# A fused attention and feed-forward block on one core: the transposes of the probabilities and of the next batch's x move from TensorE to the DMA queue, and the scores stay in PSUM

## The chip, the cores and the metric

One core of a Trainium2 chip runs the whole program in one launch. The metric is device time in microseconds (us). The kernel before takes 2261.73 us (median of 3 runs, 2261.62 to 2261.98).

## The reference

Input `x` is 8 x 512 x 1024 in f32. Attention has 16 heads of 64 with rotary position, a causal mask and a softmax; the feed-forward part is one 1024 x 1024 product with bias and a LoRA term (rank 16, one of 3 adapters by batch).

```
x = x + layernorm(attention(layernorm(x), Wq, Wk, Wv) @ Wo)
x = x + layernorm(layernorm(x) @ W.T + bias + lora(layernorm(x)))
attention: q, k rotated; softmax(where(causal, q k^T, -1e9) / 8) v
```

## The kernel before, in words

Every f32 operand of a product is split into a high and a low fp16 part, and each product is three fp16 matmul passes (high high, high low, low high) that add up in PSUM. Constants of the program are powers of two that keep the parts in range.

**Two phases.** Phase 1 does attention for 8 batches; for each batch there are 8 slots, one for each pair of heads, so 64 slots `g = 8 b + p`. Phase 2 goes over 32 tiles of 128 tokens: `Wo`, layer norm, feed-forward, layer norm. Batch 0 and batch 7 are written out; batches 1 to 6 are a loop of two bodies. The slot is a function of each engine's program (`slot(b, kind, p)`), so the order on each engine is the order in which it is written there, and semaphores tie the engines.

**One slot before, by engine (lines of the kernel before):**

- TensorE: the scores of pair p (L460, 24 matmuls of 128 to 512 columns, two heads at a time), the q product of the next pair (L435 to L437, 24 matmuls), in slots 1 to 4 of batches 0 to 6 eight f32 transposes of the next batch's normalised x (L425), the k product of the next pair (24 matmuls), the product of the probabilities with v for the previous pair (L480, 24 matmuls), 20 f32 transposes of this pair's probabilities (L469), and a quarter of the v product (L446 to L448, 24 matmuls). The v product is not there in slots 0 to 3 of batch 0 and in slots 4 to 7 of batch 7.
- VectorE (DVE): for eight score blocks ("units": 4 query blocks of 128 times 2 heads, widths 512, 384, 128, 256) the mask, the scale and the row's extreme in one pass from PSUM to SBUF (L807); the low part of v (L692); the reciprocal of the row sums (L722); the drain of q (L698, L699: a product with the cosines and a shuffle of partitions); layer-norm statistics of the next x tile (L669 to L674) and the low parts of its transposes (L686); the drain of k; `qk_low` of q (L705), the low part of the output (L716), five low parts of the transposed probabilities (L711), `qk_low` of k (L705), and the normalised x (L679).
- ScalarE (ACT): the high part of v (L989), eight exponentials with their row sums in SBUF (L1050), and the high parts: x (L984), q and k (L996), output (L1005), probabilities (L1000).
- GpSimd (POOL): eight multiplications of the exponentials by the reciprocals (L1131), the rotation of q and of k (two f32 passes each, L1122 and L1124), and one power for the layer norm (L1118).
- SP: issues all DMAs: the next x tile and the store of a pair's output (L335). In batch 7 it loads `Wo` at slot 0 and the feed-forward weight at slot 6, and at slot 7 what phase 2 needs (`phase2_loads`, with the first attention output at L331).

The scores of slot g + 1 wait for `qk_low` of k, the last link of the chain: k product, DVE drain, POOL rotation, ACT high part, DVE low part. In batch 7 the maxima of the two late weights are taken (L620, two passes of 2048 columns in each of two slots), GpSimd reduces them over the partitions (L1114), and the weights are split (ACT L978, DVE L663).

Of the kernel before, what the change touches and what calls it, by code (L numbers as in the profile page):

```python
# [52 lines left out]
Q_ORDER = (3, 2, 0, 1)  # L53
S_OFF = {3: 0, 2: 512, 0: 896, 1: 1024}
S_LEN = 1280
UNITS = [(j, a) for j in Q_ORDER for a in range(2)]
# [6 lines left out]
PT_GROUPS = (  # L63
# [5 lines left out]
)  # L69
PT_ROW = {0: ((0, 0), (2, 0)), 1: ((1, 0), (3, 0)), 2: ((4, 0), (4, 256)), 3: ((1, 384), (3, 384))}  # L70
NG = len(PT_GROUPS)

BANK_O = 7
BANK_XT = (5, 6)
# [15 lines left out]
W_V, W_Q, W_K, W_O, W_F = range(5)  # L90


def sandwich_kernel(nc, x, wq, wk, wv, wo, wf, bias, lora_a, lora_b, starts, consts, out):
# [7 lines left out]
    with ExitStack() as ctx:  # L101
# [12 lines left out]
        raw2 = arena2[:, :].rearrange("p (k n) -> p k n", k=KT)  # L114
        raw_r1 = region[1][:, :, :, :].rearrange("p k h n -> p (k h n)").bitcast(F32).rearrange(
            "p (k n) -> p k n", k=KT)
        w_raw = {W_V: raw1, W_Q: raw_r1, W_K: raw1, W_O: raw2, W_F: raw2}

        x_ring = arena2[:, 0:4096].rearrange("p (t d) -> p t d", t=ST)

# [5 lines left out]
        scores = arena1[:, 4096:4096 + 2 * S_LEN].rearrange("p (a n) -> p a n", a=2)  # L126
        pt = half(arena1[:, 6656:6656 + 2 * S_LEN], ("p (h g q) -> p h g q", dict(h=2, g=NG)))
# [15 lines left out]
        row_sum = sb("row_sum", [PART, 8], F32)  # L143
        row_inv = sb("row_inv", [PART, 8], F32)
# [72 lines left out]
        exp_done = sem("exp_done")  # L217
        inv_done = sem("inv_done")
        norm_done = sem("norm_done")
        pt_done = sem("pt_done")  # L220
        pt_high = sem("pt_high")
        pt_low = sem("pt_low")
# [83 lines left out]
        def unit_sb(j, a):  # L306
            return scores[:, a, S_OFF[j]:S_OFF[j] + 128 * (j + 1)]

# [4 lines left out]
        def _(sp):  # L313
            def load_raw(w, c):
                sp.dma_start(w_raw[w][:, KC * c:KC * (c + 1), :],
                             raw_dram[w][:, KC * c:KC * (c + 1), :]).then_inc(raw_in[w][c], 16)
# [33 lines left out]
            def slot(b, kind, p):  # L350
                first, last_b = kind == 0, kind == B - 1
                g = 8 * b + p
                if not last_b and p < ST:

                    sp.wait_ge(xt_done, 8 * b + 2 * p + 2)
                    sp.dma_start(x_ring[:, p, :], x_v[b + 1, p]).then_inc(x_in[p], 16)
                if last_b and p == 0:

                    sp.wait_ge(xt_done, 8 * B)
                    sp.wait_ge(qk_done[1], PAIRS * (B - 1))  # L360
                    sp.wait_ge(v_done, 8 * (B - 1))
                    for c in range(CHUNKS):
                        load_raw(W_O, c)
                if last_b and p == 6:
                    for c in range(CHUNKS):

                        sp.wait_ge(w_low_done, CHUNKS * W_O + c + 1)
                        load_raw(W_F, c)
                if last_b and p == PAIRS - 1:
                    phase2_loads()  # L370
                if not (first and p == 0):

                    sp.wait_ge(o_low, g)
                    if p == 0:
                        store_o(b - 1, PAIRS - 1, 1)
                    else:
                        store_o(b, p - 1, (p - 1) % 2)

# [5 lines left out]

            sp.wait_ge(o_low, PAIRS * B)
# [34 lines left out]
        def _(pe):  # L420
# [44 lines left out]
            def p_transposes():  # L465
                for bank, blocks in PT_GROUPS:
                    for n, (a, kt, j) in enumerate(blocks):
                        at = S_OFF[j] + 128 * kt
                        last = nc.tensor.transpose(ps[:, bank, 128 * n:128 * n + 128], scores[:, a, at:at + 128],  # L469
                                                   ident)  # L470
                    last.then_inc(pt_done, 1)

            def pv_products(pair):

                for kt in range(ST):
                    n = S - 128 * kt
                    for hl, vl in ((0, 0), (0, 1), (1, 0)):
                        for a in range(2):
                            grp, c = PT_ROW[kt][a]
                            last = mm(ps[64 * a:64 * a + 64, BANK_O, 128 * kt:S],  # L480
                                      v_split[:, kt, 2 * pair + a, HD * vl:HD * vl + HD], pt[:, hl, grp, c:c + n],
                                      start=(kt == 0 and hl == 0 and vl == 0), stop=(kt == ST - 1 and hl == 1))
# [27 lines left out]
            def slot(b, kind, p):  # L510
# [10 lines left out]
                need(pe, pt_low, NG * g)  # L521
# [4 lines left out]
                if has_qk:  # L526
                    if p == PAIRS - 1:
                        need(pe, xt_low, 8 * b + 16)
# [698 lines left out]
```

## Time and profile before

| | us |
|---|---|
| median of 3 runs | 2261.73 |
| the profiled execution, its own time | 2262.72 |
| its span in the trace | 2260.9 |
| TensorE busy, share of the span | 2151.5, 95% |
| VectorE busy | 1386.0, 61% |
| ScalarE busy | 791.6, 35% |
| GpSimd busy | 773.7, 34% |
| granted TensorE clock, mean | 0.978 |

The page of the profile has busy times, then the span in slices, then the chain of work that ended last, then the costliest groups. Busy time says which engine is nearly full, the slices say where, and a timeline of one slot says which wait ends last there.

### The profile page before, as it was taken

What the parts mean: (1) busy time and instruction counts of PE and PEld (TensorE: products, weight loads), DVE (VectorE), ACT (ScalarE), POOL (GpSimd) and SP (SyncE); (2) the same over time, 40 slices, a digit from 0 to 9 for tenths busy, and PEclk for the clock granted to TensorE, in tenths of its full rate; (3) what the DMA queues carried; (4) which work ended last, traced back from release to release, by engine and by line L of the source; (5) the groups of instructions that cost most, each with busy time, mean ns of one, the idle gap of its engine ahead of it and who ended that gap; (6) DMA issues with size and microseconds to landing.
All of it is one profiled execution on the core that took longest, in us unless ns stands there. A gap on an engine that the chain in (4) does not pass through costs nothing.

```text
span 2260.9 us, 35372 instructions
## 1 busy us (share of the span) xinstructions
PE 2151.5 (95%) x12928; PEld 1104.9 (49%) x12928; DVE 1386.0 (61%) x3295; ACT 791.6 (35%) x1797; POOL 773.7 (34%) x905
## 2 busy tenths in 40 slices
PE   3979999999999999999999998779999999999997
PEld 1445555555555555555555554444444444444443
DVE  6776566676576576566567565675555555555554
ACT  4544444444344444444444443532111111111111
POOL 0245455464554545455454544520000000000000
PEclk8999999999999999999999999979999999999999
DMA  7000010010010010010001020041433333423232
GB/s 294 1 29 15 20 43 11 24 34 19 24 31 24 10 43 24 10 44 20 15 29 33 15 85 10 20 177 47 121 94 84 97 82 97 117 64 114 62 79 56
DMA packets 98772, 125.47 MB, mean 55 GB/s; under 512 B 71745, under 2 KB 71745, under 8 KB 97570
## 3 DMA queue, kind: packets, MB, share of 16 engines
q1 hardware_dynamic: 98594, 123.12, 18.0%
q8 instruction: 109, 1.79, 0.3%
q14 instruction: 69, 0.57, 0.1%
HBM read 72.77 MB, written 33.55 MB: 47 GB/s over the span
## 4 chain that ended last, share of the span: by engine, by line
PE 90%; DVE 5%; issue 2%; POOL 1%; DMA 1%; ACT 1%; SPq 0%; POOLq 0%; DVEq 0%; ACTq 0%
PE ps L568 29%; PE ps L435 10%; PE ps L436 9%; PE ps L437 9%; PE ps L469 6%; PE ps L460 5%; PE ps L446 5%; PE ps L448 5%; PE ps L447 5%; PE ps L480 5%; PE ps L590 1%; PE ps L425 1%; POOL arena L1131 1%; DVE arena L711 1%; DVE w_part L620 1%
## 5 line engine op out<-in xcount | busy, mean ns | idle before, releaser
L1131 POOL TENSOR_TENSOR arena<-arena,row_inv 128x512 f32<-128x512 f32 (+3 forms) x512 | 357.9, 735 | 651.2 <-DVE row_inv L722 651.2
L435 PE MATMUL ps<-arena,region 128*128 128x512 f16 x1024 | 389.5, 380 | 0.0
L436 PE MATMUL ps<-arena,region 128*128 128x512 f16 x1024 | 388.9, 380 | 0.0
L437 PE MATMUL ps<-arena,region 128*128 128x512 f16 x1024 | 388.5, 379 | 0.0
L568 PE MATMUL ps<-region 128*128 128x512 f16 x1536 | 341.2, 383 | 8.5 <-ACT arena L1083 4.6
L807 DVE CUSTOM_DVE_ANT_0 arena<-ps,con,pow 128x512 f32<-128x512 f32 (+3 forms) x512 | 246.5, 547 | 162.1 <-PE ps L460 161.9
L568 PE MATMUL ps<-region,arena 128*128 128x512 f16 x1536 | 337.3, 379 | 0.0
L1050 ACT ACTIVATE arena<-arena,neg_max 128x512 f32<-128x512 f32 (+3 forms) x512 | 280.0, 548 | 99.3 <-DVE neg_max L807 99.3
L698 DVE TENSOR_TENSOR rotated<-ps,con 128x512 f32<-128x512 f32 x128 | 88.5, 691 | 266.7 <-PE ps L437 266.7
L568 PEld LDWEIGHTS ps<-region 128*128 128x128 f16 x1536 | 151.2, 99 | 193.5 <-issue 10.3
L1083 ACT ACTIVATE arena<-ps,sm 128x1024 f32<-128x1024 f32 x64 | 77.0, 1204 | 477.2 <-DVE sm L883 477.2
L568 PEld LDWEIGHTS ps<-region,arena 128*128 128x128 f16 x1536 | 149.2, 98 | 174.1 <-issue 0.8
L996 ACT ACTIVATE qk_high<-rotated 128x512 f16<-128x512 f32 x128 | 82.6, 645 | 422.8 <-POOL rotated L1124 422.8
L1167 POOL TENSOR_TENSOR sm<-sm,con 128x1 f32<-128x1 f32 x64 | 35.1, 548 | 508.1 <-DVE sm L876 508.1
L446 PE MATMUL ps<-region,arena 128*128 128x512 f16 x512 | 195.0, 381 | 11.8 <-DVE region L663 11.8
L711 DVE SCALAR_TENSOR_TENSOR arena<-ps,arena 128x512 f16<-128x512 f32 x320 | 196.5, 678 | 0.0
L447 PE MATMUL ps<-region,arena 128*128 128x512 f16 x512 | 195.1, 381 | 0.0
L448 PE MATMUL ps<-region,arena 128*128 128x512 f16 x512 | 194.9, 381 | 0.0
L1122 POOL TENSOR_TENSOR swapped<-swapped,con 128x512 f32<-128x512 f32 x128 | 173.3, 1354 | 43.5 <-DVE swapped L699 35.9
L1124 POOL TENSOR_TENSOR rotated<-rotated,swapped 128x512 f32<-128x512 f32 x128 | 173.4, 1355 | 10.0
L866 DVE BATCH_NORM_STATS2 st<-ps 128x6 f32<-128x512 f32 x128 | 82.8, 689 | 151.9 <-PE ps L568 140.6
L1000 ACT ACTIVATE arena<-ps 128x512 f16<-128x512 f32 x320 | 163.4, 609 | 4.5 <-PE ps L469 4.5
(121 smaller groups left out, 2668.2 us busy)
## 6 DMA issues: line engine op xcount, KB each, us to landing
arena<-x SPq DMA_DIRECT2D x32, 512.0 KB, 3.8
attn_scratch<-o_st SPq DMA_DIRECT2D x64, 256.0 KB, 2.2
region<-attn_scratch SPq DMA_DIRECT2D x8, 2048.0 KB, 8.8
v_split<-x SPq DMA_DIRECT2D x32, 512.0 KB, 4.2
out<-v_split SPq DMA_DIRECT2D x32, 512.0 KB, 5.1
arena<-wv SPq DMA_DIRECT2D x4, 1024.0 KB, 13.6
region<-wq SPq DMA_DIRECT2D x4, 1024.0 KB, 18.6
arena<-wk SPq DMA_DIRECT2D x4, 1024.0 KB, 5.5
```

Source lines behind the costliest of these rows:

```text
L435: mm(o, w[:, k, 0, cols], xnt[par][:, k, 0, :], start=(k == 0), stop=False)
L436: mm(o, w[:, k, 0, cols], xnt[par][:, k, 1, :], start=False, stop=False)
L437: last = mm(o, w[:, k, 1, cols], xnt[par][:, k, 0, :], start=False, stop=(k == KT - 1))
L446: mm(o, xnt[par][:, k, 0, tok], region[2][:, k, 0, cols], start=(k == 0), stop=False)
L447: mm(o, xnt[par][:, k, 0, tok], region[2][:, k, 1, cols], start=False, stop=False)
L448: last = mm(o, xnt[par][:, k, 1, tok], region[2][:, k, 0, cols], start=False, stop=(k == KT - 1))
L568: last = mm(ps[:, bank + c, :], stationary(k, hl), w[:, k, wl, 512 * c:512 * c + 512], start=(k == 0 and hl == 0 and wl == 0), stop=final)
L711: v.scalar_tensor_tensor(pt[:, 1, grp, :], ps[:, PT_GROUPS[grp][0], :], P_UP, pt[:, 0, grp, :], ALU.mult, ALU.subtract).then_inc(pt_low, 1)
L807: v.tensor_tensor_reduce(out=unit_sb(j, a), in0=unit_ps(j, a), in1=causal[:, 512 - width:512], scale=pow2[:, S_NEG:S_NEG + 1], scalar=HIGH ...
L1050: s.activation(unit_sb(j, a), unit_sb(j, a), ACT.Exp, bias=neg_max[:, n:n + 1], scale=-1.0, accum_out=row_sum[:, n:n + 1]).then_inc(exp_do ...
L1124: gp.tensor_tensor(rotated[which][:, :], rotated[which][:, :], swapped[which][:, :], ALU.add).then_inc(rot_done[which], 1)
L1131: gp.tensor_tensor(unit_sb(j, a), unit_sb(j, a), row_inv[:, n:n + 1].broadcast_to([PART, 128 * (j + 1)]), ALU.mult).then_inc(norm_done, 1)
```

## The change

- The 20 transposes of a slot's probabilities leave TensorE. The high and low parts are now formed before the transposition: ScalarE and VectorE read the exponentials in PSUM, multiply by the reciprocal of the row sum (times 2^14) and write fp16 blocks `p_split`; SP then issues two DMA transposes of 128 x 2560 fp16 (20 blocks of 128 x 128 each) into `pt`, after the previous pair's product with v has ended.
- Scores, mask and exponentials stay in PSUM: L842 of the kernel after (L807 before) writes its result where it read it, and the exponential does so too.
- GpSimd's eight multiplications a slot are gone.
- The eight x transposes of slots 1 to 4 leave TensorE: ScalarE makes the high part of the normalised x (1024 columns), VectorE the low part in the next slot, and SP issues two DMA transposes of 128 x 1024 fp16.
- The ring of four x tiles becomes one tile, so that the next x tile is loaded once the low part of the last is made.
- The product with v is cut at block borders: 36 matmuls of 128 or 256 columns for 24 of 128 to 512; the sum of columns is the same.
- The order of the units is (2, 0, 3, 1) by query block; the output bank is 6, which two units of scores also use.
- On VectorE the k drain comes before the statistics of x, and both `qk_low` come after the low part of the output.
- The space for the late weights is halved: two chunks of four at a time. `Wo` chunks 0, 1 load at slot 0 and 2, 3 at slot 1 of batch 7, and 0, 1 again at slot 4; the feed-forward weight's at slots 5 and 6, and 0, 1 again after the last transposes. Their maxima are taken after the low parts of the probabilities, for `Wo` in slots 1 and 2 in place of 0 and 1.

```diff
-Q_ORDER = (3, 2, 0, 1)
+Q_ORDER = (2, 0, 3, 1)
...
+READY = (2, 2, 4, 4, 5, 6, 7, 8)
+PV_PIECES = {0: ((0, 2), (2, 2)), 1: ((1, 1), (2, 2)), 2: ((2, 2),), 3: ((3, 1),)}
...
 SP, slot:
+                    for hl, src in enumerate((xn_high_t, xn_low_t[:, :])):
+                        sp.wait_ge(xn_split[hl], n)
...
+                        sp.dma_start_transpose(xnt[1 - bp][:, :, hl, tok], src).then_inc(xnt_in[hl], 16)
...
+                    sp.dma_start(x_tile, x_v[b + 1, p]).then_inc(x_next_in, 16)
+                if not (first and p == 0):
+                    sp.wait_ge(pv_done, g)
+                for hl in range(2):
+                    sp.wait_ge(p_done[hl], 8 * g + 8)
+                    sp.nop(nofuse=True)
+                    sp.dma_start_transpose(pt[:, hl], p_split[:, hl].rearrange("p a n -> p (a n)")).then_inc(
+                        pt_in[hl], 16)
...
 PE, slot:
-                need(pe, masked, 8 * g + 8)
-                if not last_b and 1 <= p <= ST:
-                    need(pe, xn_done, 4 * b + 4 + p)
-                    for hh in range(2):
-                        x_transposes(p - 1, hh, BANK_XT[hh])
...
                 if not (first and p == 0):
+                    need(pe, p_done[1], 8 * g + 4)
                     need(pe, v_low, v_before(kind, p, b))
+                    for hl in range(2):
+                        need(pe, pt_in[hl], 16 * g)
                     pv_products((p - 1) % PAIRS)
-                need(pe, norm_done, 8 * g + 8)
...
-                p_transposes()
...
 DVE:
+            def p_low_part(g, n):
+
+                j, a = UNITS[n]
+                need(dve, p_done[0], 8 * g + READY[n])
+                v.scalar_tensor_tensor(unit_p(j, a, 1), unit_ps(j, a), row_inv[:, n:n + 1], unit_p(j, a, 0),
+                                       ALU.mult, ALU.subtract).then_inc(p_done[1], 1)
...
-                    v.tensor_tensor_reduce(out=unit_sb(j, a), in0=unit_ps(j, a), in1=causal[:, 512 - width:512],
+                    v.tensor_tensor_reduce(out=unit_ps(j, a), in0=unit_ps(j, a), in1=causal[:, 512 - width:512],
...
+                if not last_b and 1 <= p <= ST:
+                    xn_low_part(4 * b + p - 1)
+                inverse(g)
                 if has_qk:
                     qk_drain(0, g + 1, bank)
...
+                need(dve, pt_in[1], 16 * g)
+                for n in range(len(UNITS)):
+                    p_low_part(g, n)
+                if last_b and p in (1, 2):
+                    part_max(W_O, 2 * (p - 1))
+                    part_max(W_O, 2 * (p - 1) + 1)
...
 ACT, slot:
+                need(act, pt_in[0], 16 * g)
+                for n in range(len(UNITS)):
+                    p_high_part(g, n)
...
+                if not last_b and p < ST:
+                    xn_high_part(4 * b + p)
...
 POOL, slot:
-                for n in range(len(UNITS)):
-                    normalise(g, n)
```

On VectorE, slot 2 of an odd batch (first body of the loop), between the masks and the drain of k, before:

```order
L722 RECIPROCAL row_inv<-row_sum 128x4 [waits exp_done]
L698 TENSOR_TENSOR rotated<-ps,con 128x512 [waits q_done]
L699 STREAM_SHUFFLE swapped<-ps 128x512
...
L669 BN_STATS bn<-arena 128x6 [waits x_in3]
L669 BN_STATS bn<-arena 128x6
...
L686 TENSOR_TENSOR arena<-ps,arena 128x4x128 [waits xt_high]
...
L698 TENSOR_TENSOR rotated<-ps,con 128x512 [waits k_done]
```

and after:

```order
L714 TENSOR_TENSOR xn_low_t<-arena 128x1024 [waits xnt_low_in,xn_high_done]
...
L757 RECIPROCAL row_rec<-row_sum 128x8 [waits exp_done]
L759 TENSOR_SCALAR row_inv<-row_rec 128x8 [waits recip_done]
L732 TENSOR_TENSOR rotated<-ps,con 128x512 [waits q_done]
L733 STREAM_SHUFFLE swapped<-ps 128x512
...
L746 SCALAR_TENSOR_TENSOR arena<-ps,row_inv,arena 128x384 [waits p_high_done]
L746 SCALAR_TENSOR_TENSOR arena<-ps,row_inv,arena 128x128 [waits p_high_done]
...
L746 SCALAR_TENSOR_TENSOR arena<-ps,row_inv,arena 128x256 [waits p_high_done] x2
L732 TENSOR_TENSOR rotated<-ps,con 128x512 [waits k_done]
L733 STREAM_SHUFFLE swapped<-ps 128x512
```

The low part of x and the eight low parts of the probabilities now stand ahead of the drain of k (`rotated` and `swapped`); the statistics (BN_STATS) have gone behind it.

On the SP queue, one slot of the same loop body before (it loads the next x tile and stores the output of the last pair):

```order
L356 ISA [waits xt_done]
L356 DMA arena<-x 128x1024
L335 ISA [waits o_low]
L335 DMA attn_scratch<-o_st 128x1024
```

and after:

```order
L368 DMA_TRANSPOSE arena<-arena 128x8x128 [waits xn_high_done]
L368 DMA_TRANSPOSE arena<-xn_low_t 128x8x128 [waits xn_low_done]
L374 ISA [waits xn_low_done]
L374 DMA arena<-x 128x1024
L376 REGISTER_ALU
L378 ISA [waits pv_done]
L380 DMA_TRANSPOSE arena<-arena 128x20x128 [waits p_high_done]
L380 DMA_TRANSPOSE arena<-arena 128x20x128 [waits p_low_done]
L341 ISA [waits o_low]
L341 DMA attn_scratch<-o_st 128x1024
```

SP now waits for four more events in each such slot and issues four transposes between the load and the store.

## Rows read from the trace of the kernel before

**Rows 1.** Stretches: length, busy PE, PEld, DVE, ACT, POOL; PEclk, DMA share, GB/s.

```profile
98.40:271.60 173.20, 158.78 (x1034) 86.12 (x1035) 112.27 (x298) 74.87 (x202) 88.89 (x100) 0.96 0.06 21
271.60:1323.80 1052.20, 1051.43 (x6913) 562.48 (x6912) 681.16 (x1752) 468.36 (x1248) 532.42 (x600) 1.00 0.08 25
1323.80:1490.70 166.90, 140.20 (x909) 74.23 (x909) 111.24 (x250) 71.01 (x177) 84.19 (x85) 0.93 0.15 58
1490.70:1516.20 25.50, 13.88 (x93) 9.52 (x94) 19.32 (x53) 9.18 (x24) 5.86 (x9) 0.57 0.40 139
```

**Rows 2.** The chain that ended last, in order of time, from one slot's scores on.

```profile
841.64 1.74 PE ps L460 x24
...
848.66 0.87 PE ps L425 x8
...
854.71 1.75 PE ps L480 x24
856.46 2.33 PE ps L469 x20
...
863.98 1.74 PE ps L460 x24
```

**Rows 3.** Timeline of DVE in that slot (start us, us, what, idle before).

```profile
842.64 0.75 DVE L807 CUSTOM_DVE_ANT_0 arena<-ps,con,pow 128x512 f32<-128x512 f32 x1 [2.75 <-PE ps L460]
...
846.41 0.69 DVE L692 SCALAR_TENSOR_TENSOR v_split<-ps,v_split 128x512 f16<-128x512 f32 x1
...
848.70 0.69 DVE L698 TENSOR_TENSOR rotated<-ps,con 128x512 f32<-128x512 f32 x1 [1.51 <-PE ps L437]
...
850.02 1.25 DVE L669 BATCH_NORM_STATS2 bn<-arena 128x6 f32<-128x512 f32 x2
...
854.75 0.69 DVE L698 TENSOR_TENSOR rotated<-ps,con 128x512 f32<-128x512 f32 x1 [1.74 <-PE ps L437]
...
860.73 0.68 DVE L705 TENSOR_TENSOR qk_low<-rotated,qk_high 128x512 f16<-128x512 f32 x1
```

**Rows 4.** Timeline of ACT in that slot.

```profile
843.43 0.72 ACT L1050 ACTIVATE arena<-arena,neg_max 128x512 f32<-128x512 f32 x1 [1.16 <-DVE neg_max L807]
...
847.31 0.49 ACT L1050 ACTIVATE arena<-arena,neg_max 128x256 f32<-128x256 f32 x1
...
857.09 2.56 ACT L1000 ACTIVATE arena<-ps 128x512 f16<-128x512 f32 x5
```

**Rows 5.** Timeline of POOL in that slot.

```profile
857.89 1.27 POOL L1124 TENSOR_TENSOR rotated<-rotated,swapped 128x512 f32<-128x512 f32 x1
```

**Rows 6.** Phase 2's low part of x, whole span (busy us, mean ns).

```profile
L925 DVE TENSOR_TENSOR arena<-arena 128x1024 f16<-128x1024 f32 x32 | 39.2, 1225 | 37.6 <-ACT arena L1093 37.6
```

**Rows 7.** Phase 2: the SP queue's two transposes of 128 x 1024 fp16.

```profile
1604.51 2.60 SPq L396 DMA_TRANSPOSE arena<-arena  x2
```

**Rows 8.** The stretch of a microsecond in which their DMA work ended.

```profile
1608.00:1609.00 1.00, 1.00 (x6) 0.49 (x5) 0.00 (x0) 0.91 (x1) 0.00 (x0) 1.00 0.38 70
```

**Rows 9.** DVE in batch 0, slot 1: masks and q's drain after an idle TensorE.

```profile
120.99 0.75 DVE L807 CUSTOM_DVE_ANT_0 arena<-ps,con,pow 128x512 f32<-128x512 f32 x1 [1.02 <-PE ps L460]
...
129.14 0.69 DVE L698 TENSOR_TENSOR rotated<-ps,con 128x512 f32<-128x512 f32 x1 [4.20 <-PE ps L437]
```

**Rows 10.** DVE in batch 7: maxima of two weight chunks, and the split of two.

```profile
1353.76 4.45 DVE L620 TENSOR_REDUCE w_part<-arena 128x1 f32<-128x2048 f32 x2
...
1455.48 4.73 DVE L663 SCALAR_TENSOR_TENSOR region<-arena,pow,region 128x2048 f16<-128x2048 f32 x2
```

**Rows 11.** POOL in batch 7, slot 2: q's rotation, the reduction, k's rotation.

```profile
1379.18 1.27 POOL L1124 TENSOR_TENSOR rotated<-rotated,swapped 128x512 f32<-128x512 f32 x1
1386.48 0.41 POOL L1114 PARTITION_ALL_REDUCE w_max<-w_pmax  x1 [6.03 <-issue]
1394.06 1.25 POOL L1122 TENSOR_TENSOR swapped<-swapped,con 128x512 f32<-128x512 f32 x1 [7.17 <-issue]
```

**Rows 12.** The chain that ended last, at the end of slot 63.

```profile
1507.17 8.87 DMA region<-attn_scratch
```

More of the change, by code:

```diff
@@ L304, in unit_ps, with unit_p, raw_of @@
             return ps[:, S_BANK[j][a], c:c + 128 * (j + 1)]
-        def unit_sb(j, a):
-            return scores[:, a, S_OFF[j]:S_OFF[j] + 128 * (j + 1)]
+        def unit_p(j, a, hl):
+            return p_split[:, hl, a, S_OFF[j]:S_OFF[j] + 128 * (j + 1)]
+        def raw_of(w, c, again):
+            if w in w_raw:
+                return w_raw[w][:, KC * c:KC * (c + 1), :]
+            return raw_late[c + 2 if w == W_F and again else c % 2]
         block = ctx.enter_context(nc.Block())
@@ L383, in _ @@
             over_batches(sp, batch)
+            for hl in range(2):
+                sp.wait_ge(pt_in[hl], 16 * PAIRS * B)
+            for c in (0, 1):
+                load_raw(W_F, c, again=True)
             sp.wait_ge(o_low, PAIRS * B)
@@ L463, in score_products @@
                         last.then_inc(s_done, 1)
[L465 to L471, printed above, removed]
             def pv_products(pair):
                 for kt in range(ST):
-                    n = S - 128 * kt
                     for hl, vl in ((0, 0), (0, 1), (1, 0)):
[L478 to L482, printed above, removed]
+                        for j, nq in PV_PIECES[kt]:
+                            at = S_OFF[j] // 128 + kt
+                            step = (S_OFF[j + 1] - S_OFF[j]) // 128 if nq == 2 else 1
+                            for a in range(2):
+                                blocks = pt[:, hl, NB * a + at:NB * a + at + (nq - 1) * step + 1:step, :]
+                                last = mm(ps[64 * a:64 * a + 64, BANK_O, 128 * j:128 * (j + nq)],
+                                          v_split[:, kt, 2 * pair + a, HD * vl:HD * vl + HD], blocks,
+                                          start=(kt == 0 and hl == 0 and vl == 0 and j == 0), stop=(kt == ST - 1 and hl == 1))
                 last.then_inc(pv_done, 1)
@@ L538, in slot @@
                 if not (first and p == 0):
+                    need(pe, p_done[1], 8 * g + 4)
                     need(pe, v_low, v_before(kind, p, b))
+                    for hl in range(2):
+                        need(pe, pt_in[hl], 16 * g)
                     pv_products((p - 1) % PAIRS)
-                need(pe, norm_done, 8 * g + 8)
-                if not last_b and 1 <= p <= ST:
-                    need(pe, xt_low, 8 * b + 8 + 2 * p)
-                p_transposes()
                 if v_slot(kind, p):
@@ L556, in _ @@
             over_batches(pe, batch)
-            pe.wait_ge(pt_low, NG * PAIRS * B)
+            for hl in range(2):
+                pe.wait_ge(pt_in[hl], 16 * PAIRS * B)
             pe.wait_ge(o_low, PAIRS * B - 1)
@@ L964, in step @@
                 if kind == 0:
[L965 to L966 removed]
+                    split_low(W_F, 2, LATE_ORDER[2])
+                    split_low(W_F, 3, LATE_ORDER[3])
             over_tiles(dve, step)
@@ L1066, in slot @@
                     o_evac(g - 1, (p - 1) % 2, stored)
-                for grp in range(NG):
-                    pt_evac(grp, g)
                 if has_qk:
                     qk_high_part(1, g + 1)
+                if not last_b and p < ST:
+                    xn_high_part(4 * b + p)
             def batch(b, kind):
@@ L1156, in slot @@
                     rotate(1, g + 1)
+                if not last_b and p < ST:
+                    ln_rstd(p, 4 * b + 4 + p)
             def batch(b, kind):
```

208 lines of the change are left out of this document (104 added, 104 removed), and 5 rows, old and new, of the table PT_GROUPS.

## The prediction

> **What bounds the kernel now.** I read the busy times by stretch first, because the program has parts with different limits. In batches 1 to 6 TensorE is busy 1051.43 of 1052.20 us at full clock, while DVE has 681, POOL 532, ACT 468 [rows 1]: there the kernel is worth exactly the TensorE work in it. Batch 0 (158.78 of 173.20) and batch 7 (140.20 of 166.90) have gaps, and slot 63 with the hand-over to phase 2 is 25.5 us for 13.9 of TensorE work at clock 0.57 [rows 1]. Second, the chain in order of time for one slot: 22.34 us from scores to scores (863.98 - 841.64), of which 0.87 are x transposes, 2.33 the transposes of the probabilities, 1.75 the product with v, 1.74 the scores [rows 2]; the rest is the three projections. Third, timelines of DVE, ACT and POOL in the same slot, to see what the other engines can be asked for when TensorE's share shrinks [rows 3 to 5].
>
> Phase 2 (744.7 us from 1516.2) and the first 98.4 us are touched by nothing that I can price; I leave them.
>
> **The sum against TensorE, batches 1 to 6.** Removed: 48 x 2.33 = 111.8 and 24 x 0.87 = 20.9, together 132.7 us. The product with v gets 36 matmuls for 24 but the same 3840 pairs of columns; the 24 take 1.75 us, 0.46 ns a column, which is 2.4 GHz with nothing to spare for a fixed cost [rows 2]. I take 0 for the cut; at worst 12 more instructions at 0.02 us add 0.24 us a slot (11 us), and that goes into the range. A slot becomes 22.34 - 3.20 = 19.14 us, and one without x transposes the same. So 1052.2 becomes 919.5.
>
> **Does the rest fit into 19.14 us?** Times from the start of a slot (T). Masks start at 1.0 and v's low part follows at 4.77 [rows 3]; nothing says that writing to PSUM costs more, so I keep that. The low part of x, 1024 columns, is priced by phase 2's same pass, 1.23 [rows 6]: about 6.6 with v's part (0.6). Exponentials: the first needs two masks now, so starts near 2.0, and the eight took 843.43 to 847.8, 4.4 us [rows 4]: 6.4. The two small operations of the inverse end near 6.9. DVE would wait for q's product until 7.1 anyway (848.70 - 841.64) [rows 3], so up to here the added work is hidden in an old wait. The drain of q takes 1.32 (848.70 to 850.02) [rows 3]: 8.4. Eight high parts on ACT: 512 columns cost 0.51 [rows 4], and I take 0.85 ns a column and 0.08 to 0.15 each, 3.0 us: 7.0 to 10.0. Eight low parts on DVE at 0.6 us for 512 columns (the v part, 846.41 on, [rows 3]) are 3.2 us: 11.7. The k product ends so that its drain can start at 13.11 - 0.87 = 12.24 [rows 3]. DVE is ready 0.5 us early.
>
> From k's drain to the next scores the old links are: drain start to end of rotation 859.16 - 854.75 = 4.41 [rows 3, 5], a high part (0.6), a low part (0.68 [rows 3]), hand-offs 0.5: 6.2 us. The statistics and both other low parts lie under POOL's rotation. That gives 12.24 + 6.2 = 18.4 for the earliest next scores against TensorE's 19.14: slack **0.7 us**. TensorE stays the bound, but the chain of the k half has come from 3 us behind to 0.7 us behind it.
>
> **The queue.** SP must wait for the end of the previous product with v (T + 14.0) and then issues both big transposes. Sixteen blocks of 128 x 128 were issued in 2.60 us and their DMA work ended about 4.0 us after the first issue (1604.51 to 1608.4) [rows 7, 8]. Forty blocks: by the rate of issue 2.5 x 2.60 + 1.4 = 7.9 us, by plain scaling 10.0 us; I take 9, so landing at T + 23. The first who needs them is ACT's high part of the next slot (the source buffer is free only then) at 26.1, for the high half alone, then DVE's low part at 27.5, then TensorE at 31.3. Spare: 4 us. The x transposes (2.60 us of issue) and the x load sit at T + 1 to 8 of a slot, when the queue is idle; the x tile must land before the statistics at 13.6. The output store waits until about 20.5, and its buffer is needed two slots later. I cost all of it at nothing; if this cover is gone, the rival on transposes says what it costs.
>
> The Trainium skill (DMA: Bandwidth & Descriptors, the table of quirks) gives 261 GB/s for DMA transposes with a non-contiguous middle dimension: an estimate by it is 5.0 us for the 1.31 MB of a slot. It would only widen the spare time; no run here shows that rate, the trace stands at 16 blocks in 4.0 us.
>
> **Batch 0.** Slots 0 to 3 have no v product, so TensorE's work (14.0 us) ends before the chain (18.4), and idle time lowers the clock. In slot 1 before, q's drain came 8.15 us after the masks instead of 6.06 [rows 9, 3]: 2.1 us for a clock at the lower level after an idle gap. I take 18.7 for slot 0, 18.4 + 2.1 for slots 1 to 3, 19.14 + 2.1 for slot 4, and 3 x 19.14: 158.9, which is 14.3 less than 173.2. Bounds: no clock cost, 150; twice the cost, 167.
>
> **Batch 7.** Here the change adds work ahead of k's drain. Slot 0: 19.1. Slot 1: two maxima of 4.45 us [rows 10] come after the low parts, 11.7 + 4.4 = 16.1 for the drain, + 6.2 = 22.3 (21.5 before, when they filled an old wait). Slot 2: maxima again until 16.3; POOL's gap of 6.03 us before the reduction starts when q's rotation ends, now T + 11.0, so the reduction is at 17.0 and k's rotation at 17.0 + 0.4 + 7.2 = 24.6 [rows 11]; + 4.2 = 28.8, against 31.4 before, because q's rotation no longer stands behind POOL's multiplications. Slot 3: two us of small operations ahead of the drain and a low clock, 21. Slots 4 and 5: a split of two chunks (4.73 [rows 10]) after the low parts, drain at 16.8, 23 and 24.5. Slot 6: maxima, 23.7. Sum 162.4: 4.5 less. Slot 63: DVE reaches the LoRA clearing at 14.8 instead of 11.7 after its start, and SP has two transposes and a store ahead of the attention loads, so the load of 8.87 us [rows 12] is issued at about T + 20.5, not 16.5: 4 us **more**. The repeated half of the feed-forward weight lands behind it (T + 42) and is split first at T + 46.
>
> **The sum.** 132.7 + 14.3 + 4.5 - 4 = 147.5 less. The profiled execution took 2262.7, so 2115.2; the median of the runs is 1.0 below it: **2114 us**.
>
> **The rivals.**
>
> *The other engines bind in every slot.* The slack is 0.7 us on the way through k's drain and 0.5 ahead of it. For: masks and exponentials now write PSUM, no row of this trace shows either engine doing so, and DVE's low parts wait for ACT's high parts in pairs. Against: reads of PSUM are in nearly every row and cost no visible extra. From both sides: 0 less or more by a few hundredths each, and at most a doubled fixed part. ACT's two widths (0.72 at 512, 0.49 at 256 columns) leave 0.26 us of fixed time [rows 4]; eight more on DVE and eight more on ACT move the inverse from 6.9 to about 9.1, low parts to 13.8, the slot to 20.0. With a slower POOL beside DVE's two-operand passes, 20.5. So plus 0.4 to 1.3 us in 50 slots: 2135 to 2180, middle **2150**. The Trainium skill (VectorE: DVE Perf Modes, the errata table) gives DVE 120 cycles of fixed cost with PSUM as source against 58 for SBUF; if a destination there cost as much, an estimate by that page is 0.5 us for the eight masks, which DVE's old wait for q nearly hides. No row here shows such a destination.
>
> *The transposes bind, and it ends slower than before.* One buffer for `pt` and one for `p_split` make a loop: low half lands, DVE writes the next low parts (3.2 us), both halves are issued again. If forty blocks take D, a slot can't be shorter than D + 3.2 plus a wait or so. It starts to matter at D = 13.5 (T + 14.0 to 27.5) and eats the whole gain near D = 18.8, slot 22.0. That is 1.9 to 2.4 times my two values. At D = 24 the slots take 27 us: 64 x 8 = 510 more than forecast, over 2600; just past the turn, at D = 20, **2330**. For: 128 x 2560 is a form that the trace has not, and reads and writes of one big transpose may not spread as the small ones do. Against: rate and issue time of the same kind of transfer leave half the queue empty. A mild form (D of 14 to 18) would give 2130 to 2250.
>
> *The clock holds or the ends cost nothing:* batch 0 without low clock and slot 63 without the late load give **2102**.
>
> *The change does less than it says:* x transposes for a batch still wait for their last tile in slot 4; if a late x load stalls DVE ahead of `qk_low` in slots 1 to 3, 18 slots pay a us or two: 2135 to 2150, inside the first rival's numbers.
>
> **How the numbers follow.** My forecast 0.66 (its own range 2104 to 2128); other engines or a late x load bind 0.22; transposes bind mildly 0.04, with loss 0.04; better than the forecast 0.04. The range 2102 to 2158 leaves out the upper part of the first rival, the transposes, and little below. A measurement tells 0.2%, 4.5 us, from no change. Faster 0.95, same 0.01, slower 0.04.
>
> **What would show it.** Right: in batches 1 to 6 TensorE still has no gap, scores to scores 19.1 us, and the product with v still 1.75 to 1.8; k's drain starts by T + 12.3 without DVE being late; waits of ACT, DVE or TensorE for the DMA transposes are absent; POOL has two rotations a slot and nothing else but a power; no matmul of 128 x 128 f32 remains after batch 0's start. Wrong: TensorE waits at the scores for `qk_low` in each slot (first rival; the length of masks and exponentials says who), or DVE's first low part waits for a DMA (second), or the landing time of a big transpose is over 13 us. In batch 7 slot 2 should be 29 us and slot 63 about 29.5; if the low clock spreads there, the ends give less than I say.

## The result and the profile after

| | before | changed kernel |
|---|---|---|
| median of 4 runs | 2261.68 us | 2132.61 us (2130.05 to 2133.54) |
| profiled execution: own time, span | 2262.7, 2260.9 us | 2133.54, 2131.7 us |
| ratio of the times | 1 | 0.9428 (95% interval 0.9411 to 0.9444) |

Faster by 129 us, where 148 were forecast. The busy time by stretch, cut at the same events as [rows 1], tells where the other 18 us are (columns: stretch and its length, then busy us of PE, PE's weight loads, DVE, ACT, POOL, then granted clock, DMA share, GB/s):

```profile
98.20:257.90 159.70, 142.77 (x924) 69.96 (x924) 122.73 (x317) 81.39 (x222) 44.34 (x36) 0.90 0.49 95
257.90:1189.30 931.40, 926.16 (x6337) 457.35 (x6336) 738.23 (x1872) 507.24 (x1368) 265.98 (x216) 1.00 0.55 110
1189.30:1354.10 164.80, 127.27 (x853) 63.17 (x852) 117.97 (x271) 76.46 (x198) 37.44 (x29) 0.89 0.52 122
1354.10:1386.00 31.90, 9.87 (x96) 7.45 (x96) 20.29 (x56) 9.39 (x27) 0.40 (x1) 0.66 0.79 233
1386.00:2131.70 745.70, 726.89 (x3712) 343.62 (x3712) 397.56 (x853) 118.03 (x100) 52.69 (x96) 0.99 0.34 90
```

Batch 0 came out 0.8 us over the forecast, batches 1 to 6 11.9 over, batch 7 2.4, slot 63 2.6 and phase 2 0.8 (phase 2's first matmul starts at 1386.22, so the fourth stretch is cut 0.2 us too early: slot 63 is 32.1 us). Batches 1 to 6 are still TensorE's: 926.16 of 931.40 us. The difference of 11.9 has two parts. 44 of their 48 slots take 19.26 us, from scores to scores in the chain of waits (start, length, what):

```profile
782.09 1.74 PE ps L497 x24
...
794.29 1.77 PE ps L511 x36
796.06 0.32 PE ps L483
...
801.34 1.74 PE ps L497 x24
```

The next scores start 19.25 us later, against 22.34 in [rows 2]. The 36 matmuls of the cut product take 1.77 us for 1.75, and the first matmul of the v projection behind them holds 0.32 us of the chain, where each later one holds 0.22. So the cut and the hand-over behind it cost 0.12 us a slot, 5.8 us in 48. The same 0.32 stood in the trace before, where the q projection follows the scores:

```profile
843.37 0.32 PE ps L435
```

Behind the product with v it did not show there, since the f32 transposes came in between; they took their cover away with them. The other part sits in four slots around the loop's two turn-rounds, where its body ends and starts again (batch 2 to 3 and 4 to 5): 21.84, 20.89, 22.00 and 19.46 us, 7.1 us over 4 x 19.26. In the kernel before the last slots of the body were 0.49 and 0.41 us over their neighbours, so 6.2 us of it are new.

Inside a slot, DVE's timeline (start, us, engine, line, operation; in brackets its idle time before and what ended it), as [rows 3] before; scores started at 782.02:

```profile
783.00 0.63 DVE L842 CUSTOM_DVE_ANT_0 ps<-ps,con,pow 128x384 f32<-128x384 f32 x1 [1.77 <-PE ps L497]
...
784.62 0.76 DVE L842 CUSTOM_DVE_ANT_0 ps<-ps,con,pow 128x512 f32<-128x512 f32 x1
...
787.38 1.21 DVE L714 TENSOR_TENSOR xn_low_t<-arena 128x1024 f16<-128x1024 f32 x1
...
789.15 0.69 DVE L732 TENSOR_TENSOR rotated<-ps,con 128x512 f32<-128x512 f32 x1 [0.24 <-PE ps L474]
...
790.39 3.75 DVE L746 SCALAR_TENSOR_TENSOR arena<-ps,row_inv,arena 128x384 f16<-128x384 f32 x8
794.33 0.69 DVE L732 TENSOR_TENSOR rotated<-ps,con 128x512 f32<-128x512 f32 x1 [0.19 <-PE ps L474]
...
799.06 0.69 DVE L739 TENSOR_TENSOR qk_low<-rotated,qk_high 128x512 f16<-128x512 f32 x1
```

q's drain waits for TensorE (0.24), k's drain waits for TensorE (0.19), and the low part of k ends at 799.7 while the next scores come at 801.27. ACT's exponentials in the same slot, as [rows 4], with the probabilities now in PSUM:

```profile
785.81 0.67 ACT L1090 ACTIVATE ps<-ps,neg_max 128x512 f32<-128x512 f32 x1
...
787.13 0.47 ACT L1090 ACTIVATE ps<-ps,neg_max 128x256 f32<-128x256 f32 x1
```

A mask of 512 columns takes 0.76 us into PSUM and took 0.75 into SBUF [rows 3], and the eight masks with what belongs to them take 3.78 us (783.00 to 786.78) for 3.77 (842.64 to 846.41): on VectorE the destination in PSUM costs nothing. An exponential is 0.67 for 0.72 and 0.47 for 0.49 [rows 4]. The Trainium skill (ScalarE: Activation LUTs, Step-by-step: what each stage is for) says that of two destinations PSUM is the quicker one for ScalarE. The trace goes that way, by 0.02 to 0.05 us each, but it does not separate the two ends: the source of the exponentials moved to PSUM as well. POOL is busy 410.6 us of the span. The big DMA transposes on SP's queue, first in the timeline of this slot, then in the summary of their line (all 128 of them: duration of the issue in ns, who waited, us to landing):

```profile
796.23 6.25 SPq L380 DMA_TRANSPOSE arena<-arena  x2
```

```profile
L380 SPq DMA_TRANSPOSE arena<-arena x128: 2912/3082/3935, 110.2 to 1370.8; - x128
...
  PE ps L511: 8.3, 1
...
DMA to landing us min/median/max: 4.8/5.0/7.4
```

In this slot the second is issued 3.1 us behind the first and lands 5.0 after that: 8.1, at T + 22.3 (T is the start of the slot's scores), where I had 9 and T + 23. The longest landing is 7.4, so a pair can take over 10. TensorE waited for one once, in slot 63.

### The profile page after: what moved, and what is told of

Same layout as the page of the kernel before. It is cut to its first block, busy times and chain, and to the rows that moved or that the text cites. A ratio compares the mean times of both kernels' runs of the same rounds, so it can differ in the third digit from the quotient of the medians.

```text
span 2131.7 us, 34075 instructions
## 1 busy us (share of the span) xinstructions
PE 1994.7 (94%) x12192; PEld 971.1 (46%) x12192; DVE 1460.8 (69%) x3459; ACT 842.7 (40%) x1961; POOL 410.6 (19%) x393
## 4 chain that ended last, share of the span: by engine, by line
PE 90%; DVE 5%; issue 2%; POOL 1%; DMA 1%; ACT 1%; SPq 0%; POOLq 0%; DVEq 0%; ACTq 0%
PE ps L595 30%; PE ps L472 11%; PE ps L473 10%; PE ps L474 10%; PE ps L497 6%; PE ps L483 5%; PE ps L484 5%; PE ps L485 5%; PE ps L511 5%; PE ps L617 1%; DVE w_part L647 1%; DVE arena L746 1%; PE ps L628 1%; PE ps L627 1%; DVE region L691 1%
## 5 line engine op out<-in xcount | busy, mean ns | idle before, releaser
L842 DVE CUSTOM_DVE_ANT_0 ps<-ps,con,pow 128x384 f32<-128x384 f32 (+3 forms) x512 | 246.9, 555 | 133.6 <-PE ps L497 133.4
L1162 POOL TENSOR_TENSOR swapped<-swapped,con 128x512 f32<-128x512 f32 x128 | 162.2, 1267 | 909.0 <-DVE swapped L733 901.9
L1090 ACT ACTIVATE ps<-ps,neg_max 128x384 f32<-128x384 f32 (+3 forms) x512 | 258.2, 510 | 89.8 <-DVE neg_max L842 89.8
L746 DVE SCALAR_TENSOR_TENSOR arena<-ps,row_inv,arena 128x384 f16<-128x384 f32 (+3 forms) x512 | 239.6, 542 | 1.0 <-ACT arena L1035 1.0
L1035 ACT ACTIVATE arena<-ps,row_inv 128x384 f16<-128x384 f32 (+3 forms) x512 | 221.2, 543 | 40.9 <-DVE row_inv L759 40.9
L1164 POOL TENSOR_TENSOR rotated<-rotated,swapped 128x512 f32<-128x512 f32 x128 | 163.8, 1279 | 10.0
L472 PEld LDWEIGHTS ps<-arena,region 128*128 128x128 f16 x1024 | 100.6, 98 | 130.4 <-issue 18.5
L474 PEld LDWEIGHTS ps<-arena,region 128*128 128x128 f16 x1024 | 100.9, 99 | 123.1 <-issue 4.1
L473 PEld LDWEIGHTS ps<-arena,region 128*128 128x128 f16 x1024 | 100.8, 98 | 114.6 <-issue 2.2
```

The lines of the kernel that those rows point to most:

```text
L472: mm(o, w[:, k, 0, cols], xnt[par][:, k, 0, :], start=(k == 0), stop=False)
L473: mm(o, w[:, k, 0, cols], xnt[par][:, k, 1, :], start=False, stop=False)
L474: last = mm(o, w[:, k, 1, cols], xnt[par][:, k, 0, :], start=False, stop=(k == KT - 1))
L746: v.scalar_tensor_tensor(unit_p(j, a, 1), unit_ps(j, a), row_inv[:, n:n + 1], unit_p(j, a, 0), ALU.mult, ALU.subtract).then_inc(p_done[1], 1)
L842: v.tensor_tensor_reduce(out=unit_ps(j, a), in0=unit_ps(j, a), in1=causal[:, 512 - width:512], scale=pow2[:, S_NEG:S_NEG + 1], scalar=HIGH ...
L1035: s.activation(unit_p(j, a, 0), unit_ps(j, a), ACT.Copy, scale=row_inv[:, n:n + 1]).then_inc(p_done[0], 1)
```

## The experiments

Four variants of the changed kernel were run. Their ratios are to the kernel before as measured beside them (2261.27 us, median of 9). Slot lengths, in us, from the first matmul of one slot's scores to that of the next:

| kernel | batch 0, slots 0 to 4 | a slot of batches 1 to 6 | turn-round: last slot, first slot (twice) | batch 7, slots 0 to 6 |
|---|---|---|---|---|
| changed | 19.45, 20.05, 20.26, 20.37, 21.85 | 19.26 | 21.84, 20.89; 22.00, 19.46 | 19.26, 22.25, 30.39, 21.77, 22.42, 24.61, 24.12 |
| TensorE transposes back | 18.72, 19.48, 17.86, 17.85, 21.48 | 21.48 | 22.33, 21.48; 22.05, 21.48 | 21.48, 22.25, 28.59, 23.56, 22.41, 23.71, 23.65 |
| one block | 18.72, 19.50, 19.47, 20.48, 21.90 | 19.26 | 19.47, 20.42; 19.75, 21.41 | 19.26, 22.25, 30.20, 21.75, 22.42, 24.60, 24.11 |
| statistics first | 20.74, 22.10, 21.15, 20.87, 22.00 | 19.83 in most with statistics (8 of 24 are 0.1 to 1.5 longer), 19.26 | 21.76, 20.27; 21.96, 21.36 | 19.26, 22.26, 28.58, 21.46, 22.45, 24.44, 24.03 |
| behind the turn | 19.45, 20.28, 20.38, 20.43, 21.88 | 19.26 | 19.26, 19.42; 19.28, 19.74 | 19.26, 22.24, 30.25, 21.69, 22.41, 24.59, 24.10 |

### TensorE transposes back

```diff
                     pv_products((p - 1) % PAIRS)
+                need(pe, p_done[1], 8 * g + 8)
+                for n in range(20):
+                    nc.tensor.transpose(ps[:, 5, 128 * (n % 4):128 * (n % 4) + 128], ident, ident)
```

> The changed kernel, plus 20 f32 transposes of the identity on TensorE behind each product with v (2.33 us in a slot of the kernel before), once the product's result has been read from its bank. Theory (TensorE's work alone sets the slot in batches 1 to 6): a slot goes from 19.26 to 21.6 us, batches 1 to 6 from 931.4 to about 1043, the whole to 2240 to 2265, most of the change's gain gone, although ACT, DVE, POOL and the DMA queue do exactly what they do in the changed kernel. Rival (the other engines set 19.26, TensorE only fills it): the 1.4 us between the low part of k and the next scores takes up part of the 2.33, a slot is 20.2 to 20.6 and the whole about 2190 to 2205.

The wait in the edit is for the slot's eight low parts and not for the product's result: one of them reads bank 5, into which the transposes write.

Measured: 2234.62 us (ratio to the kernel before 0.9883, interval 0.9865 to 0.9901), a slot 21.48 us, none of batches 1 to 6 with less. The chain of this kernel:

```profile
829.12 1.77 PE ps L511 x36
830.88 2.34 PE ps L572 x20
...
838.40 1.74 PE ps L497 x24
```

TensorE's work alone sets the slot: of 2.33 us put back, 2.22 came out as time. The missing 0.11 is the hand-over: with the f32 transposes between the cut product and the projection, the projection's first matmul holds 0.21 us (at 833.22) and not 0.32, and 19.26 + 2.34 becomes 21.48 and not 21.60. So 0.10 of the 0.12 us is not the 12 additional matmuls but what follows them. Why the hand-over costs this, no run tells.

The total is below my 2240 to 2265. Batches 1 to 6 took 1032.6 us and not 1043: 5 us are the covered hand-over, and 5.7 are the turn-rounds, which lie 1.4 us over 4 x 21.48 where they lay 7.1 over 4 x 19.26 (more on this under "Behind the turn"). And batch 0 took 159.8 us, as in the changed kernel, although 20 transposes were added in each of its slots. There TensorE has no v product in slots 0 to 3 and idles, and the filler keeps it busy. The stretch of one slot in the changed kernel, then in this one (columns as above, the clock third from the end):

```profile
137.70:157.90 20.20, 16.44 (x108) 8.10 (x108) 16.16 (x42) 10.55 (x28) 6.01 (x5) 0.84 0.67 130
```

```profile
136.20:154.10 17.90, 16.42 (x132) 9.57 (x130) 16.28 (x42) 10.54 (x28) 6.03 (x5) 1.00 0.69 148
```

And q's drain on DVE's timeline in these two slots, in the same order:

```profile
147.23 0.69 DVE L732 TENSOR_TENSOR rotated<-ps,con 128x512 f32<-128x512 f32 x1 [2.33 <-PE ps L474]
```

```profile
142.93 0.69 DVE L735 TENSOR_TENSOR rotated<-ps,con 128x512 f32<-128x512 f32 x1 [0.54 <-PE ps L474]
```

With 20 useless transposes the slot is 2.4 us **shorter**: the clock stays at 1.00 (2.4 GHz) instead of 0.84 on average, and q's drain waits 0.54 us for its product where it waited 2.33. 17.85 us is also the measured length of the chain through the other engines: the scores of these slots wait for k's low part (1.48 us).

### One block

```diff
-                    sp.dma_start_transpose(pt[:, hl], p_split[:, hl].rearrange("p a n -> p (a n)")).then_inc(
-                        pt_in[hl], 16)
+                    if first and p == 0:
+                        ...
+                    else:
+                        sp.dma_start_transpose(pt[:, hl, 0:1], p_split[:, hl, 0, 0:128]).then_inc(pt_in[hl], 16)
```

> Each big DMA transpose after the first slot's moves one block of 128 x 128 only and leaves the other 19 out (the transposed probabilities are stale for them); all waits stay. Theory: the two slots at the loop's turn-round that are 2.6 and 2.7 us too long (21.84, 22.0; one after it 20.89) are long because the instructions of the loop's start are fetched beside the big transposes; without these the turn-rounds cost under 1 us each (about 7 us less together), slot 63 loses its wait for the transposes and the load behind them (5 to 8 us less), the other slots stay at 19.26: about 2117 to 2121. If the 0.12 us that each slot lies above 19.14 is traffic of the transposes, they also go to 19.14 or so, 6 us more: 2111 to 2115. Rival (the transposes are hidden everywhere, the turn-round is long for another reason): 2126 to 2133.

Measured: 2123.71 us (2122.22 to 2126.29), ratio 0.9390 (0.9376 to 0.9405), 8.9 us under the changed kernel, between my 2117 to 2121 and the rival's 2126 to 2133. The slots stayed at 19.26 to a hundredth: the 0.12 us is no traffic of the transposes. The turn-rounds fell by 3.1 us together, not by 7: smaller gaps were left, now in the first slot, of 1.01 us at one turn-round and 2.00 at the other. Batch 0 is 1.9 us shorter, which I did not expect and have not followed up. My expectation for slot 63 failed: it lost 1.2 us, not 5 to 8. The load of the attention took 8.17 us for 9.36, but it is issued no sooner, for what stands ahead of it is not the transposes (below).

### Statistics first

```diff
-                if has_qk:
-                    qk_drain(1, g + 1, 1 - bank)
                 if not last_b and p < ST:
                     need(dve, x_next_in, 16 * (4 * b + p + 1))
                     ln_stats(p, 4 * b + 4 + p, x_tile)
+                if has_qk:
+                    qk_drain(1, g + 1, 1 - bank)
+                    qk_low_part(0, g + 1)
                 if not (first and p == 0):
                     o_evac(g - 1, (p - 1) % 2)
                 if has_qk:
-                    qk_low_part(0, g + 1)
                     qk_low_part(1, g + 1)
```

> The order of VectorE of the kernel before, in the changed kernel: x's statistics ahead of k's drain (1.7 us later), k's first low part behind the statistics. Theory (1.4 us lie between the end of k's low part and the scores in each slot): in the slots with statistics the scores come 0.3 us late or more, 28 slots, 5 to 12 us in all: 2138 to 2145. Rival (the slack is as small as the 0.7 us I reckoned with): 1.0 us and more in each of 24 slots, 2157 or more. Other rival (the move was worth nothing, since POOL's rotation and the drain's cover take it up): within 2 us of 2132.6.

Measured: 2153.56 us (2151.7 to 2155.4), ratio 0.9526 (0.9513 to 0.9539): 21 us more, above my 2138 to 2145. DVE, POOL and PE of one slot of this kernel, where q's drain was at 308.89:

```profile
313.79 1.28 DVE L697 BATCH_NORM_STATS2 bn<-arena 128x6 f32<-128x512 f32 x2
315.48 0.68 DVE L732 TENSOR_TENSOR rotated<-ps,con 128x512 f32<-128x512 f32 x1
...
320.55 0.69 DVE L739 TENSOR_TENSOR qk_low<-rotated,qk_high 128x512 f16<-128x512 f32 x1 [2.57 <-ACT qk_high L1030]
```

```profile
316.89 1.62 POOL L1162 TENSOR_TENSOR swapped<-swapped,con 128x512 f32<-128x512 f32 x1 [3.97 <-DVE swapped L733]
```

```profile
321.60 0.34 PE L497 MATMUL ps<-qk_high 64*128 64x384 f16 x2 [0.51 <-DVE qk_low L739]
```

From q's drain to k's drain are 6.59 us for 5.18 in the changed kernel, and POOL's first pass of the rotation takes 1.62 us for 1.26: it now runs beside DVE's low parts of q and of the output, as it did in the kernel before (1.64 at 856.18), and not beside the statistics. Together that is 1.41 + 0.36 = 1.77 us later. The low part of k waits for that rotation, and the scores wait 0.51 for the low part. 0.57 us a slot came out, so the slack was 1.2 us. My 0.3 a slot had left out POOL, and it had taken all 1.4 us behind k's low part as slack, though TensorE starts 0.36 us after that low part ends (321.24 to 321.60). 24 slots with 0.57 are 14 us, the other differences in batches 1 to 6 add 2.6, batch 0 gives 5 (there the chain is the bound, so most of the delay comes out), and batch 7 gives 2.3 back, most of it in slot 2, where the clock did not fall. These are differences of the profiled executions, 18 us in all; the medians are 21 apart. The order in the change is worth 21 us of its 129, though the diff shows two moved calls.

### Behind the turn

```diff
                 if not (first and p == 0):
                     sp.wait_ge(pv_done, g)
+                if kind == 2 and p == PAIRS - 1:
+                    sp.wait_ge(s_done, 3 * g + 4)
```

> In the last slot of the loop's body alone, the big transposes wait for the next slot's scores, so that they run behind the loop's turn-round instead of beside it. Theory (the fetch of the loop's first instructions shares the DMA engines with the transposes): the gap of about 2.5 us at each of two turn-rounds goes, the following slot may wait up to 1 us for its transposes: 2126 to 2130. Rival (the gap comes from the jump itself or from something else): no change, 2131 to 2136, or a us or two more.

Measured: 2124.99 us (2117.99 to 2126.58), ratio 0.9390 (0.9376 to 0.9403): 7.6 us under the changed kernel, one under my 2126 to 2130, and the fastest here that leaves nothing out. 6.5 us of it lie in the four slots of the turn-rounds; the profiled execution also started its first scores 1.0 us sooner (97.2 for 98.2), which the wait does not touch. First the stretches of a microsecond in the changed kernel at the first turn-round (columns as in the first table of stretches: PE's busy time stands behind the comma, the clock third from the end, then DMA share and GB/s):

```profile
565.00:566.00 1.00, 1.00 (x5) 0.29 (x3) 0.00 (x0) 0.00 (x0) 0.00 (x0) 1.00 1.88 185
566.00:567.00 1.00, 0.06 (x1) 0.00 (x0) 0.00 (x0) 0.00 (x0) 0.00 (x0) 1.00 1.29 19
567.00:568.00 1.00, 0.00 (x0) 0.00 (x0) 0.00 (x0) 0.00 (x0) 0.00 (x0) 1.00 0.53 100
568.00:569.00 1.00, 0.42 (x6) 0.31 (x8) 0.00 (x0) 0.60 (x1) 0.00 (x0) 1.00 1.28 290
...
570.00:571.00 1.00, 1.00 (x10) 0.40 (x6) 1.00 (x7) 0.45 (x1) 0.00 (x0) 0.50 0.90 133
```

In the timelines of SP and ACT:

```profile
560.95 7.08 SPq L380 DMA_TRANSPOSE arena<-arena  x2
...
568.29 0.60 ACT L1023 ACTIVATE v_split<-ps 128x512 f16<-128x512 f32 x1 [4.53 <-issue]
```

From about 566.1 to 568.3 no engine of the core does anything, and ACT's wait ends with "issue": it waited for nothing that the profile shows. TensorE's gap ahead of the scores is 2.5 us. After it the clock is at 0.50 (1.2 GHz) for some three microseconds, and the next slot takes 20.89. At the second turn-round the gap is 2.7 us, the clock stays at 1.00, and the next slot takes 19.46. In the kernel with the wait, the first place again:

```profile
565.00:566.00 1.00, 1.00 (x11) 0.38 (x11) 0.00 (x0) 0.41 (x1) 0.00 (x0) 1.00 0.12 25
566.00:567.00 1.00, 1.00 (x18) 0.63 (x16) 0.40 (x1) 0.18 (x1) 0.00 (x0) 1.00 0.02 8
567.00:568.00 1.00, 1.00 (x10) 0.41 (x6) 1.00 (x7) 0.41 (x1) 0.00 (x0) 1.00 0.29 62
568.00:569.00 1.00, 1.00 (x6) 0.39 (x4) 1.00 (x7) 1.00 (x6) 0.00 (x0) 1.00 1.14 216
```

TensorE has no gap, the clock stays at 1.00, and the transposes run behind the scores. What else runs there is in the view of DMA queues, for 563 to 570 us of the changed kernel (packets, MB, share of 16 engines):

```profile
q1 hardware_dynamic: 4567, 1.31, 119.3%
q8 instruction: 2, 0.03, 1.9%
q14 instruction: 4, 0.03, 1.3%
```

Packets of the queues called "instruction" run there too, beside those of the transposes, whose queue is over 100% of 16 engines in this view. Shown is that holding SP's queue back removes the gap. That the gap is a fetch of the loop's first instructions behind those packets is my reading of it, and three other observations bear on it:

- The gap needs the jump back. At the end of batch 6, where the loop ends and the same transposes run at the same place, the slot takes 19.25 us. The jump without transposes costs little: 0.49 and 0.41 us in the kernel before.
- With the TensorE transposes back, TensorE reaches the turn 2.2 us later and the DMA transposes stand where they stood. The gap is 0.8 and 0.5 us for 2.5 and 2.7, and the next scores come at T + 22.33 and 22.05, for 21.84 and 22.00 in the changed kernel. So what TensorE waits for comes at about T + 22 in both kernels, a time that goes with the transposes (issued from T + 14.2 to about T + 21.4) and not with the moment at which TensorE jumps.
- The run without 19 of 20 blocks supports it by half: the gaps shrank to 1.01 and 2.00 us. There the output store and x's load, no longer behind long transposes, fell on the microseconds ahead of the first of them (DMA share 1.09 from 563 to 564 us in that kernel), while the wait of this kernel holds these back too.

In the changed kernel the store and x's load are issued at T + 21.5 and T + 22.6, at the end of the gap or behind it, so there the transposes alone stand ahead of it. How much the store and the load do in the kernel "one block", no run tells, nor whether any large transfer does this or only a transposing one.

**What was not tried.** These have no run: the big transposes done twice (how near they are to binding), plain copies in their place, the late VectorE work of batch 7 behind k's drain with the first attention load ahead of slot 63's transposes, and the filler on TensorE in batch 0 alone, on top of the last kernel. The last is what I would do first: by the table, slots 0 to 3 with the filler and slot 4 at 19.26 would be 8.8 us shorter together (93.17 for 101.98), which is worked out and not measured. Some 1.3 us of it are doubtful: the kernel "one block" has 18.72 and 19.50 in slots 0 and 1 without any filler.

## Why the prediction was right, and where it was off

The mechanism of the likeliest case came true: TensorE bounds batches 1 to 6, and what leaves it is what is gained. The number did not fall in that case's own range: 2132.6 is 18.6 us over the forecast of 2114 and 4.6 over the top of 2104 to 2128, and lies in the whole range of 2102 to 2158. Every stretch came out longer than forecast, batches 1 to 6 most (11.9 us). By its steps:

- **TensorE's sum** (132.7 us in batches 1 to 6, 19.14 a slot). Right as mechanism, shown by the first experiment. "I take 0 for the cut; at worst 0.24 a slot" was 0.12, 5.8 us in all, of which 0.02 is the product and 0.10 the hand-over. "0.46 ns a column, which is 2.4 GHz with nothing to spare" was misread: at the same clock six projection matmuls of 512 columns take 1.29 us in that trace (859.23 to 860.52), 0.42 ns a column and 1.61 us for 3840, so 0.14 us of the 1.75 was something else. The cut added 0.02. And the 0.10 could have been read from the trace before, behind the scores.
- **Does the rest fit.** Expected 0.7 us of slack at the scores; it was 1.2 (by "statistics first") to 1.4 (19.26 - 17.85, the latter from batch 0). PSUM as destination cost nothing: masks and exponentials took what they took before or less. k's drain began at T + 12.3 (794.33 - 782.02) against 12.24, waiting 0.19 for TensorE: DVE was ready 0.2 early, not 0.5, since its eight low parts took 3.75 and not 3.2 us; they began at T + 8.4, as reckoned. From k's drain to the next possible scores I had 6.2 us; it was some 0.4 less (794.33 to 799.75, and 0.36 to TensorE's start).
- **The queue.** 8.1 us for both in the slot shown, between my 7.9 (by the rate of issue) and 9. No wait for their data but the one of 8.3 us in slot 63, and that not on the chain. The step that failed is "I cost all of it at nothing": at two turn-rounds the transposes go with a stop that no wait in either trace names, 7.1 us, 6.2 more than before. Holding the queue back removes the stop, and the store and the load behind them are issued only at its end; that it is a fetch of instructions is a reading. I had asked who waits for the transposes and who waits behind them on SP, but not who else uses the DMA engines. (On SP two of a slot's four transposes stand ahead of x's load and two between the load and the store, as the list of its queue shows, and not all four between them.)
- **The Trainium skill**'s rate for DMA transposes (DMA: Bandwidth & Descriptors, Latency and other measured facts), 261 GB/s, would have given 5.0 us for 1.31 MB, an estimate. The runs show 3.1 us of issue for each 0.66 MB transpose, 213 GB/s over the issue, and 8.1 us from the first issue to the last landing, 162 GB/s. The measurement decides: by the page one would have placed the landing 3 us too early.
- **Batch 0.** 159.7 for 158.9. The clock cost of 2.1 us in a slot was 2.4 in slot 2, by the pair above, and the chain 17.85 instead of 18.4: two small errors that cancel, so that the closeness of the sum is in part luck. Slot 0 was 0.8 over and slots 1 to 3 0.8 under together.
- **Batch 7.** Slots forecast 19.1, 22.3, 28.8, 21, 23, 24.5, 23.7; they were 19.26, 22.25, 30.39, 21.77, 22.42, 24.61, 24.12. Only slot 2 is off by more than a microsecond. DVE and POOL there:

```profile
1239.60 0.69 DVE L732 TENSOR_TENSOR rotated<-ps,con 128x512 f32<-128x512 f32 x1 [2.17 <-PE ps L474]
...
1249.65 0.41 POOL L1154 PARTITION_ALL_REDUCE w_max<-w_pmax  x1 [6.03 <-DVE w_pmax L655]
1257.14 1.25 POOL L1162 TENSOR_TENSOR swapped<-swapped,con 128x512 f32<-128x512 f32 x1 [7.09 <-issue]
```

  POOL's gaps are the 6.03 and 7.1 of [rows 11], as used. q's drain was held for 2.17 us by its product, since after TensorE's wait of 2.92 us ahead of the scores the clock stood at 0.50 from 1232 to 1235 us. In the kernel "statistics first" TensorE waited 2.94 at the same place, the clock stayed at 1.00, that drain waited 0.54, and the slot took 28.58, within 0.3 of my number: what was missing is a fall of the clock. It came in the traces of three kernels after a wait of 2.92 us (30.39, 30.20 and 30.25 for the slot) and not in that of "statistics first".
- **Slot 63.** 32.1 for 29.5; the reason was named right (DVE late, so the store and the loads behind it late), the size was not. The chain there:

```profile
1362.40 3.76 DVE arena L746 x8
1366.16 4.38 DVE w_part L647 x2
...
1370.71 0.92 DVE arena L813
...
1373.56 0.61 DVE o_st L751
...
1374.19 0.36 SPq L341
...
1376.72 9.36 DMA region<-attn_scratch
```

  The clearing starts at T + 16.6 (T is 1354.1), not 14.8: the exponentials ended at 6.8 for 6.4, DVE's low parts began at 8.3, behind ACT's first two high parts, and took 3.76. I had reckoned 7.1 and 3.2. The attention load on the chain is issued at T + 22.6, not 20.5, and took 9.36 for 8.87 [rows 12].

The rivals: "the other engines bind" would have shown scores that wait for `qk_low` in each slot; they did in batches 0 and 7 alone. It was 1.2 us away, and two moved calls bring it on (19.83). "The transposes bind" was far: 13.4 us were there from issue to need (796.23 to 809.64, DVE's first low part of the next slot), 8.1 were used. "The ends cost nothing" fell too: the clock cost 2.4 us in slot 2 of batch 0, and slot 63 is 6.6 us longer than before [rows 1].

## What to carry to other kernels

Where one engine is busy for 1051 of 1052 us, what is taken from it is what is gained, as long as the longest chain through the others is measured in the same slot; here it had 1.2 us to spare, and two calls in the wrong place would have given back 21 of 129 us. A large transfer that nobody waits for can still cost: look at the places where the program jumps back, and try a wait that moves the transfer if it falls there; here that gained 6.5 us in four slots. What is taken off an engine can also have covered something: look for the same hand-over elsewhere in the trace. Idle time of TensorE had a price of its own in batch 0: before shortening a stage in which TensorE has holes, ask whether useless work in the holes would be cheaper.

## What I had not expected of the hardware

- 20 matmuls without use made a slot 2.4 us shorter (17.86 for 20.26, slot 2 of batch 0), as the clock stayed at 1.00 instead of 0.84.
- Two big DMA transposes at the loop's turn-round go with a stop of all engines of the core for over 2 us that no wait in the trace explains; held back by 6 us, with the store and the load behind them, they go with none.
- After nearly equal idle times of TensorE (2.92 and 2.94 us, ahead of slot 2's scores in batch 7) the clock fell to 0.50 in the changed kernel's trace and stayed at 1.00 in that of "statistics first"; the slot took 30.39 and 28.58 us.
- The first projection matmul behind the product with v, or behind the scores, holds 0.10 us more of the chain than the later ones; behind f32 transposes it does not.
- POOL's pass over 512 f32 columns took 1.62 us for 1.26 where DVE's low parts of q and of the output ran beside it; beside the statistics it took 1.26.
- Exponentials with PSUM as source and destination are shorter (0.67 for 0.72 us at 512 columns) than those from and into SBUF; masks of 512 columns take 0.76 us into PSUM and 0.75 into SBUF.
